# One block in place of two: attention and feed forward of a transformer layer joined by semaphores, and half scales computed straight from PSUM

## What is computed

```
a = layernorm(x)
xn = layernorm(a) * g1 + b1
q, k = 16 heads of 8;  v = 8 "retrievals" of 8, shared by the heads
out[i, h, r] = sum_j softmax_j(q k^T)[h, i, j] * v[j, r]
comp = softmax_r([qv, out] @ Ws + bs)          # mixing of the 8 retrievals
a = a + (sum_r comp * out) @ Wf.T + bf
a = a + relu((layernorm(a) * g2 + b2) @ Wr1.T + br1) @ Wr2.T + br2
x = x + a
x = x + gelu(layernorm(x) @ ternary(W1).T + fb1) @ ternary(W2).T + fb2
ternary(w): s = max(mean(|w|), 1e-8);  w + (clip(round(w / s), -1, 1) - w)
```

## Time and profile before

| what | us |
|---|---|
| median of 3 runs (lowest, highest) | 1229.66 (1228.99, 1229.75) |
| the profiled execution | 1227.82 |
| its span, first to last instruction | 1225.9 |

### The profile page before, as it was taken

One profiled execution on the slowest core, in us unless ns is written; L12 is line 12 of the kernel. 1 busy time (PEld: TensorE's weight loads), 2 busy tenths in 40 slices (PEclk: granted clock), 3 DMA queues, 4 the chain that ended last, 5 costly groups with the idle time before them and its releaser, 6 DMA issues. The chain is left out here.

```text
span 1225.9 us, 27573 instructions
## 1 busy us (share of the span) xinstructions
PE 1168.6 (95%) x7997; PEld 542.7 (44%) x7997; DVE 950.6 (78%) x2128; ACT 756.2 (62%) x1461; POOL 955.8 (78%) x561
## 2 busy tenths in 40 slices
PE   4699999999999999999999999999999999968898
PEld 2144444444444444444444444444444444425675
DVE  7676788888888787878787888787878888767762
ACT  4066767666666766666666666666666666654443
POOL 5277898989899898988898989897978878873321
PEclk9599999999999999999999999999999999999999
DMA  5334444343444344444444443444444434330000
GB/s 129 109 65 97 94 98 105 88 103 88 109 97 106 82 95 93 99 91 95 99 91 107 94 105 79 109 98 97 97 97 96 95 81 99 68 70 1 18 26 26
DMA packets 55765, 107.14 MB, mean 87 GB/s; under 512 B 6144, under 2 KB 25056, under 8 KB 55728
## 3 DMA queue, kind: packets, MB, share of 16 engines
q0 software_dynamic: 18784, 67.70, 29.2%
q1 hardware_dynamic: 36162, 38.65, 9.9%
q10 hardware_dynamic: 782, 0.33, 0.1%
HBM read 22.51 MB, written 8.39 MB: 25 GB/s over the span
## 5 line engine op out<-in xcount | busy, mean ns | idle before, releaser
L1245 DVE TENSOR_REDUCE rowmax<-row_bank 128x1 f32<-128x512 f32 x1024 | 662.3, 684 | 185.0 <-PE row_bank L1052 180.8
L1196 ACT ACTIVATE prob<-col_bank 128x512 f32<-128x512 f32 x1024 | 554.6, 594 | 263.8 <-PE col_bank L1071 262.7
L1081 PE MATMUL out_bank<-prob,v_op 128*64 128x512 f32 x2048 | 534.5, 594 | 0.2 <-ACT prob L1196 0.2
L1355 POOL TENSOR_TENSOR addend<-prob 128x1024 f32<-128x1024 f32 x128 | 323.1, 2524 | 45.9 <-ACT prob L1196 45.9
L1355 POOL TENSOR_TENSOR quad<-prob 128x1024 f32<-128x1024 f32 x128 | 335.1, 2618 | 20.1 <-ACT prob L1196 20.0
L1052 PE MATMUL row_bank<-k_op,q_op 72*64 72x512 bf16 x2048 | 326.9, 387 | 13.4 <-DMA q_op<-q_parts 8.9
L1071 PE MATMUL col_bank<-q_op,k_op 74*64 74x512 bf16 x2048 | 317.1, 382 | 3.4 <-DMA q_op<-max_rows 2.4
L1071 PEld LDWEIGHTS col_bank<-q_op,k_op 74*64 74x64 bf16 x2048 | 118.0, 109 | 246.9 <-ACT prob L1196 208.1
L1052 PEld LDWEIGHTS row_bank<-k_op,q_op 72*64 72x64 bf16 x2048 | 122.5, 109 | 153.1 <-DVE rowmax L1245 54.9
L1081 PEld LDWEIGHTS out_bank<-prob,v_op 128*64 128x64 f32 x2048 | 152.9, 136 | 67.3 <-issue 8.0
L1360 POOL DMA_DIRECT2D quad<-addend x128 | 112.4, 878 | 77.4 <-POOL addend L1355 72.8
(11 more groups left out here) (202 smaller groups left out, 805.6 us busy)
## 6 DMA issues: line engine op xcount, KB each, us to landing
quad<-addend POOLq DMA_DIRECT2D x128, 512.0 KB, 5.4
k_op<-k_parts SPq DMA_DIRECT2D x64, 144.0 KB
q_op<-q_parts SPq DMA_DIRECT2D x192, 48.0 KB
v_op<-v_all SPq DMA_DIRECT2D x32, 256.0 KB, 5.9
q_parts<-along_parts SPq DMA_DIRECT2D x11, 192.0 KB, 2.1
k_parts<-along_parts SPq DMA_DIRECT2D x33, 64.0 KB, 2.1
out<-y_out SPq DMA_DIRECT2D x8, 256.0 KB, 2.3
q_op<-max_rows SPq DMA_DIRECT2D x64, 4.0 KB
```

Of the source, the lines that this page charges most:

```text
L1081: last = nc.tensor.matmul(out_bank[ih * VW:(ih + 1) * VW, :], v_op[slot // 2][:, t, :], outs.halves(prob[:, t, :])[:, :, ih, :], start=(t ...
L1196: nc.scalar.activation(prob[:, t, h * HALF:(h + 1) * HALF], col_bank[h][:, :], ACT.Exp).then_inc(exp_done, 1)
L1245: nc.vector.tensor_reduce(rowmax[:, parity, t, h:h + 1], row_bank[h][:, :], AX.X, ALU.max).then_inc(max_done, 1)
L1355: pool.tensor_tensor(dst, prob[:, 2 * k, :], prob[:, 2 * k + 1, :], ALU.add).then_inc(pair_done, 1)
```

## The change

The block of attention stays open, and the feed forward's instructions are added to it; so the drain and the barrier between the two go. The semaphores of both parts are now held until the end (`sems`). Where the barrier had kept memory safe, two waits are added: TensorE waits for all eight ternary steps before it projects block 1 into `mid_bank` (which lies on a `row_bank`), and ScalarE waits for GpSimd's last addition but one before it writes `onT` (which lies in `prob`). ScalarE's copy of block 1 is moved ahead of its last `take_out`, and VectorE's normalize of block 0 ahead of the sum of tiles 3 to 6. The scales are made by two instructions from PSUM instead of three.

```diff
-        v.tensor_scalar(scale[:, :, 0], bank[:, 0:2], 1.0 / (FF * DIM), 1e-8, ALU.mult,
+        v.tensor_scalar(scale[:, :, 0], bank[:, 0:2], 0.5 / (FF * DIM), 0.5e-8, ALU.mult,
                         ALU.max).then_inc(self.scale_ready, 1)
-        dve.wait_ge(self.scale_ready, 1)
-        v.tensor_scalar(scale[:, :, 1], scale[:, :, 0], -0.5, None, ALU.mult).then_inc(self.scale_ready, 1)
-        dve.wait_ge(self.scale_ready, 2)
-        v.tensor_scalar(scale[:, :, 0], scale[:, :, 0], 0.5, None, ALU.mult).then_inc(self.scale_ready, 1)
+        v.tensor_scalar(scale[:, :, 1], bank[:, 0:2], -0.5 / (FF * DIM), -0.5e-8, ALU.mult,
+                        ALU.min).then_inc(self.scale_ready, 1)
...
-        dve.wait_ge(self.scale_ready, 3)
+        dve.wait_ge(self.scale_ready, 2)
...
-def attention(nc, res, mix, outs, joined, ffw, a):
+def attention(nc, sems, block, res, mix, outs, joined, ffw, a):
...
-        block = ctx.enter_context(nc.Block())
...
                             if last and s == SLOTS - 1:
-                                pe.wait_ge(ffw.scale_ready, 1)
+                                pe.wait_ge(ffw.scale_ready, 2)
                             outs.turn_out(pe, u - 1)
...
             group(GROUPS - 1, False, True, False)
+            joined.copy(act, 1)
             outs.take_out(act, U - 1)
...
                         if last and (s, t) == (3, 5):
                             ffw.ternary(dve, 0, row_bank[0])
-                        if last and (s, t) == (3, 6):
                             joined.norm.normalize(dve, 0)
...
-def feed_forward(nc, res, mix, outs, joined, ffw, out):
+        return pair_done
+
+
+def feed_forward(nc, sems, block, res, mix, outs, joined, ffw, pair_done, out):
...
-        block = ctx.enter_context(nc.Block())
...
                     if not isinstance(k, int) or k > 1:
                         pe.wait_ge(x3_part, k - 1)
+                    else:
+                        pe.wait_ge(ffw.tern_step, 8)
                     joined.project(pe, k, mid_bank)
...
                 if live(k):
-                    joined.copy(act, k)
-                if live(k):
+                    if not isinstance(k, int) or k > 1:
+                        joined.copy(act, k)
                     joined.take(act, k, turn_bank)
                 if isinstance(k, int) and k == 1:
                     outs.take_turned(act, U - 1, G, SLOTS - 1)
                 if live(k - 1):
                     act.wait_ge(norm2.turned, k)
+                    if isinstance(k, int) and k == 1:
+                        act.wait_ge(pair_done, TB // 2 * U - 1)
                     nc.scalar.activation(onT[:, :], turn2_bank[:, :], ACT.Identity,
...
-        attention(nc, res, mix, outs, joined, ffw, args)
-        feed_forward(nc, res, mix, outs, joined, ffw, out)
+        sems = ctx.enter_context(ExitStack())
+        block = ctx.enter_context(nc.Block())
+        pair_done = attention(nc, sems, block, res, mix, outs, joined, ffw, args)
+        feed_forward(nc, sems, block, res, mix, outs, joined, ffw, pair_done, out)
```

More of the change, by code:

```diff
@@ L119, with __init__ @@
 class Projections:
-    def __init__(self, nc, ctx, res, name, ring, turned, qk, v):
+    def __init__(self, nc, ctx, sems, res, name, ring, turned, qk, v):
         def sb(what, shape, dtype=FP32):
@@ L131, in sem @@
         def sem(what):
-            return ctx.enter_context(nc.semaphore(f"{name}_{what}"))
+            return sems.enter_context(nc.semaphore(f"{name}_{what}"))
         self.nc, self.res, self.ring = nc, res, ring
@@ L544, with __init__ @@
 class BlockNorm:
-    def __init__(self, nc, ctx, res, name, src):
+    def __init__(self, nc, ctx, sems, res, name, src):
         def sb(what, shape):
@@ L607, in __init__ @@
         self.attT = ctx.enter_context(nc.sbuf_tensor("attT", [P, HALF], FP32))
-        self.norm = BlockNorm(nc, ctx, res, "norm2", res.y)
+        self.norm = BlockNorm(nc, ctx, ctx, res, "norm2", res.y)
         self.copied, self.turned, self.attT_ready = sem("att_copied"), sem("att_turned"), sem("attT_ready")
@@ L662, in prepare @@
         bank = [ctx.enter_context(nc.psum_tensor(f"prep{n}", [P, HALF], FP32)) for n in range(8)]
-        project = Projections(nc, ctx, res, "first", PAIRS_BEFORE, turned=bank[0:2], qk=bank[2:4], v=bank[4:6])
+        project = Projections(nc, ctx, ctx, res, "first", PAIRS_BEFORE, turned=bank[0:2], qk=bank[2:4], v=bank[4:6])
         tiles_before = PAIR * PAIRS_BEFORE
@@ L969, in sem @@
         def sem(name):
-            return ctx.enter_context(nc.semaphore(name))
+            return sems.enter_context(nc.semaphore(name))
         q_op, k_op, v_op, operands_in = res.q_op, res.k_op, res.v_op, res.operands_in
@@ L985, in attention @@
         out_bank, turn_bank = outs.out_bank, outs.turn_bank
-        project = Projections(nc, ctx, res, "along", 1, turned=[turn_bank], qk=[turn_bank], v=[turn_bank])
+        project = Projections(nc, ctx, sems, res, "along", 1, turned=[turn_bank], qk=[turn_bank], v=[turn_bank])
         max_in = [sem(f"max_in{s}") for s in range(SLOTS)]
@@ L1415, in feed_forward @@
         G = GROUPS - 1
-        norm2, norm3 = joined.norm, BlockNorm(nc, ctx, res, "norm3", res.x)
+        norm2, norm3 = joined.norm, BlockNorm(nc, ctx, sems, res, "norm3", res.x)
         onT, hT = sb("onT", [P, HALF]), sb("hT", [P, HT, HALF])
```

## The result

| | before | changed |
|---|---|---|
| median, us (lowest, highest; runs) | 1229.66 (1227.89, 1231.65; 9) | 1222.5 (1221.02, 1227.62; 9) |
| ratio, 95% interval | | 0.9949 (0.9938 to 0.9961) |
| the profiled execution's span | 1225.9 | 1220.2 |

The two profiled spans differ by 5.7 us, the medians by 7.2; the interval of the ratio allows 4.8 to 7.6 us.

A forecast was written before the change was run, and what follows sets the result against it. TensorE bounds the attention stretch; at the join the barrier delays GpSimd's product. Copy, scales and waits 0, product −6.24, sum −6.2 us: 1221.6 from the profiled execution, 1223.4 against the 1229.66 median, range 1220.9 to 1227.0.

The forecast's parts named there:

- The product carries the join's worth: At the join of the two blocks, GpSimd's logit product starts 6.24 us earlier and all later work moves with it.
- VectorE's sums are the new limit: Behind the removed barrier, VectorE's last output sum ends at 1099.71 and releases GpSimd's product at 1099.88.
- The normalize is held by GpSimd's addition: At the join, VectorE's early normalize ends at 1097.30, 0.85 us after GpSimd's last addition; unblocked, the gain is 0.66 larger.
- The barrier was held by a transfer nobody needed: At attention's end, GpSimd's drain held the barrier some 3 us for a transfer not needed until step 1's denominators.
- The copy and the added waits are free: ScalarE's moved 0.63 us copy fits a 0.75 us hole, and the waits of TensorE and ScalarE cost zero.
- The scales are worth nothing: VectorE is free about 3 us earlier, but a later variance step is held to the same moment: zero.
- I take zero: The scales term: zero gain, with bounds of a 2.9 us loss that disappears and a 0.9 gain later given back.
- Rival 2: Part is given back, 1 to 3.5 us, by a clock drop in step 2 or GpSimd's drain being own work; 0.21.
- signs of being wrong: Product starting at GpSimd's own end or after 1102, growing distances behind the product, or granted clock below 1 behind 1115.
- Rival 4: The clock stays low through step 3, making 1126.3 to 1140 12.9 us longer, 1236.3 in all; chance 0.05.
- Rival 1: GpSimd, not VectorE, limits at the join: product at 1098.0, 8.1 us earlier, time 1221.5; chance 0.15.
- The case that the drain was GpSimd's own work: Within the 0.21 rival: GpSimd's drain is descriptor work, so the product cannot start before 1102.4; a gain of 3.6.

The follow-up runs named there:

- e2: The changed kernel with VectorE's normalize of block 0 back behind the sum of tiles 3 to 6; 1224.01 us in its one execution.
- e5: The changed kernel with the last group's output sums for tiles 2 to 7 in one instruction right behind the scales; median 1220.24 us, ratio to before 0.9925.
- e3: The kernel before, with its two blocks and barrier, but without GpSimd's drain at the end of attention; ratio 0.996.
- e8: The changed kernel with ScalarE's copy of block 1 back behind its last output copy; 1221.56 us in its one execution.
- e1: The changed kernel with the three old scale instructions; 1220.80 us in its one execution.
- e4: The changed kernel with 20 idle turns of weights in TensorE's pause of step 2; 1223.06 us in its one execution.
- e12: The kernel before with the new two-instruction scales alone; 1229.84 us in its one execution.
- e9: The changed kernel measured once more, unaltered; median 1223.7 us, ratio to before 0.9952.
- e10: The changed kernel with one semaphore instruction more in VectorE's list, right behind the scales; 1222.33 us in its one execution.

## Why the prediction was right

- *The product carries the join's worth.* Right. Its start moved by 6.11 us (6.15 from the transfer issue), and everything behind it by the same up to step 4. Release to start was taken as 0.17 and measured 0.21.
- *VectorE's sums are the new limit.* Right: forecast 1099.71 and 1099.88 for the sums and the product, measured 1099.80 and 1100.01. e2 and e5 show it as cause: with the sums 0.7 earlier the product is 0.7 earlier, and with the sums out of the way GpSimd is the limit.
- *The normalize is held by GpSimd's addition.* Right: end forecast 1097.30, measured 1097.35; in e2 it is not held. That the change so gives away 0.7 us is shown, at the join. The order in which the records start does not always tell who is held: in rows 9 the scale-to-scale step starts 0.37 us before GpSimd's addition and still ends with it.
- *The barrier was held by a transfer nobody needed.* Right, and e3 gives its share: 3.14 of 6.15.
- *The copy and the added waits are free.* The copy: shown by e8. For the waits, TensorE's projection ran directly behind the turn and ScalarE's write came with the turn's end; neither was taken out to be tried. The denominators did not wait for their transfer: TensorE began them at 1103.67, behind its reduce.
- *The scales are worth nothing.* Right in the timing of the join (e1). Wrong by a term that I did not have: the step "I take zero" counted durations and left out that one instruction less shifts the code; 0.36 us lost, so that the end gains 5.79 in place of 6.24. The other 0.09 is the product's start.
- *The clock.* Rival 2 said that TensorE's longer pause in step 2 might bring the clock down. The dip came, and with it one of my signs of being wrong, a clock below 1 behind 1115, though the forecast stood; the growing distance of step 4 to 5 was another, and it is the stall. The pause was 2.13 us and not nearly 4, because TensorE also waited 1.30 for the addition to y before the projection; I had let it run on. The cost was zero where it fell in the changed kernel, and 1.4 to 1.6 us in e2, e3, e4 and e12, where it fell in step 3. Rival 4 itself did not come: the clock was full at the join. What the four show is a short low stretch of some 3 us at the place that rival 4 names, at about a tenth of its price.
- Rival 1, GpSimd as the limit, is what e5 makes of the kernel; the change itself did not reach it. The case that the drain was GpSimd's own work fell with the changed kernel itself, whose product starts 2.94 us behind the issue, where the old drain ended 5.3 behind it. Two readings of the rivals were loose: of the 1.9 us that rival 1 needs, the unblocked normalize is 0.66, a third and not half; and 1 us given back is 1224.4 and not 1224.7.

The medians moved by 7.2 us, 1.4 more than the end of the profiled executions, and the interval covers both. No part of the trace explains the rest, and the second measurement did not have it: with e9 the medians are 1229.62 and 1223.7, 5.9 apart. So the mechanism and its size are borne out by the distances; how near the median came to 1223.4 is in part luck.

## What to carry to other kernels

A barrier costs more than its own instructions: ask what its slowest drain waits for and whether anyone needs that yet. When it goes, list everything that the first critical instruction behind it waits for, each with its own time; the last of these is the new limit, and it may be work that could have been done in a hole that the list shows (here 3 us of sums in 2.3 us of idleness, worth another 2 us). And look for small VectorE steps beside a long GpSimd instruction. Here the `TENSOR_SCALAR` steps on 2 or 4 values per partition, from SBUF to SBUF, ended when it did (3.06, 0.51, 1.39 and 2.58 us for steps that otherwise take 0.17), and what was saved ahead of them was lost.

## What was not expected of the hardware

- One instruction more or less in VectorE's list, in an idle time, brought or took away a stall of 0.36 us in a loop 57 us later (11.31 or 10.95 us for the same work; changed kernel and e10).
- The granted clock fell to half for some 3 to 4 us where no pause of TensorE in steps 2 and 3 was longer than 2.14 us: in step 2 in five profiles, in step 3 in four, one of them with its longest pause filled (e4). Five profiles have no such dip. The kernel before is one of them, while e12, which differs from it by the scales alone, has one that cost 1.56 us. In e12 the low clock of the join ended sooner (0.94 in the window 1106 to 1108, 0.50 before), so TensorE ran ahead and its pause in step 2 was 1.46 us in place of 0.41.
- GpSimd's product was recorded as starting 0.65 us after the start of a transfer issue of 0.91 us, and took 4.82 us in place of 4.52 (e5).
